# Spreading a vector over the partitions through DRAM instead of through TensorE, in a two-stage cross-attention kernel

## The chip, the cores and the metric

The kernel runs on one core of one Trainium2 chip. The metric is the device time of one execution in microseconds.

## What is computed

For 64 independent sequences: x is 256 x 512, the context c is 256 x 256, all in float32. Two cross-attention layers follow one another, the second one with its softmax over the query axis and a layer norm:

```
Q = x Wq0 + bq0; K = c Wk0 + bk0; V = c Wv0 + bv0
x1 = x + softmax(Q K^T / sqrt(512), axis = keys) V Wo0 + bo0
q = x1 Wq1 + bq1; k = c Wk1 + bk1; v = c Wv1 + bv1
w = softmax(q k^T / sqrt(512), axis = queries)
x2 = w v + x1
out = (x2 - mean) * rsqrt(var + eps) * gamma + beta
```

The kernel multiplies the weights together beforehand. The key bias bk1 then contributes a term x1 . g1 to the score of each query, with g1 = Wq1 bk1 / sqrt(512). It differs from query to query, so it does not drop out of a softmax over the queries, and it has to be added to each of the scores. The change is about this term.

## The kernel before

One round of the program works on several sequences at once, each in another stage. With r the round, TensorE (`body` in the PE block) issues u(r+3), Pc(r+2), g(r), S1(r), S0(r+3), pred(r-1), out(r+2), v(r+1), s(r), wc(r). The other engines have bodies of their own, written out by hand in program order: ScalarE (ACT) and GpSimd (POOL) split every operand of a matmul into a high and a low float32r part (`xT_h` and `xT_l`, and so on), VectorE (DVE) does the rest of the low parts, the maxima, the residual sums and the statistics. Rounds 4 to 55 are a loop of 13 trips of 4 bodies, the rest is unrolled. Engines wait for one another by semaphores only. Each engine's queue is strictly in order: a wait holds back all that stands behind it.

Two matrices are transposed by way of DRAM, through SyncE's (SP's) queue: `move_E0(n)` waits for E0_blk, writes it in four DMAs to E0_dram, waits for them and reads PT_raw back; `move_y(n)` does the same with y_blk, y_dram and yT_raw. PT_raw becomes PT_hi (ACT) and PT_lo (POOL), the moving operand of Pc; yT_raw becomes yT_hi and yT_lo, the moving operand of v. In round r SP does load_IN(r+5), load_x(r+2), store(r-2), move_E0(r+3), move_y(r+2). Before the rounds it runs move_E0(0), (1), (2) and move_y(0), (1).

The bias term: in round r DVE computes `dot(r+1)` (L729): for each half q of the queries, x1 times g1, summed along the row, into one column of gcol[n % 2] (128 x 2: one number per query). In the scores S1 the queries lie along the free axis and the keys on the partitions, so each of the 128 partitions needs all 256 numbers. PE's `g_` (L331) makes them: it transposes the column, broadcast to 128 x 128, against the identity `ident`, twice, into PSUM bank 0; ACT's `gT_` (L550) copies the 128 x 256 result to gT in SBUF; DVE's `max1` (L744) waits for gT and for S1, adds gT to both halves of S1 and takes the negative maxima.

```
last = nc.tensor.transpose(g_bank[:, q * P:(q + 1) * P],
                           gcol[n.k % 2][:, q:q + 1].to_broadcast([P, P]), ident[:, :])
...
copy(gT[:, 0, :], g_bank[:, 0:S]).then_inc(gT_set, 1)
```

In the profile's rows L268 is the helper `product`, from which nearly all matmuls come, L337 the transposes of `g_`, L475 ACT's copies, L735 the dots, L750 the addition of gT, L787 the sum x2, L908 POOL's low parts; SP's rows are L195 (R, that is load_x), L203 and L207 (move_E0), L214 and L218 (move_y), L224 (store).

Of the kernel before, what the change touches and what calls it, by code (L numbers as in the profile page):

```python
# [4 lines left out]
P = 128  # L5
NSEQ, S, D, L = 64, 256, 512, 256
# [42 lines left out]
def build(nc, x, packed, WqT0, bq0, WkT0, WvT0, bv0, Wo0, bo0, WqT1, WkT1, bk1, Wv1, bv1, gamma, beta, out):  # L49
# [6 lines left out]
    with ExitStack() as stack:  # L56
# [6 lines left out]
        def sem(name):  # L63
            return stack.enter_context(nc.semaphore(name))

        ident = sb("ident", [P, P])
        A0 = split("A0", [P, DT, L])
        Bv = split("Bv", [P, LT, D])
        A1 = split("A1", [P, DT, L])
# [37 lines left out]
        yT_raw = sb("yT_raw", [P, NB * ST, DT, 32])  # L107
        yT = split("yT", [P, NB * ST, DT, 32])
        gcol = [sb(f"gcol{n}", [P, ST]) for n in range(2)]
        gT = sb("gT", [P, 1, S])  # L110
        srow = sb("srow", [P, S], f32r)
        nmax0, Z0 = sb("nmax0", [P, ST]), sb("Z0", [P, ST])
        rz0 = [sb(f"rz0{n}", [P, ST]) for n in range(2)]
# [4 lines left out]

        E0_dram = nc.dram_tensor("E0_dram", (NB, 32, NB, ST * LT * 32), f32, kind="Internal").ap()
        y_dram = nc.dram_tensor("y_dram", (NB, 32, NB, ST * DT * 32), f32, kind="Internal").ap()  # L120

        bank = [stack.enter_context(nc.psum_tensor(f"bank{n}", [P, 512], f32)) for n in range(8)]
        g_bank = s_bank = bank[0]
        Pc_bank = v_bank = bank[1]
        u_bank = bank[2]
        g1_b = bank[3]
# [15 lines left out]
        PT_hi, PT_lo = sem("PT_hi"), sem("PT_lo")  # L142
        Pc_full, Pc_hi, Pc_lo = sem("Pc_full"), sem("Pc_hi"), sem("Pc_lo")
        out_full, x1_set = sem("out_full"), sem("x1_set")
        g_set, g_full, gT_set = sem("g_set"), sem("g_full"), sem("gT_set")
        y_blk_set, y_blk_out, yT_in = sem("y_blk_set"), sem("y_blk_out"), sem("yT_in")
        yT_hi, yT_lo = sem("yT_hi"), sem("yT_lo")
        v_full, v_hi, v_lo = sem("v_full"), sem("v_hi"), sem("v_lo")
# [29 lines left out]
        @block.sync  # L178
        def _(sp):
            def weights(dst, src, n):  # L180
                sp.dma_start(dst[:, :, :], src).then_inc(w_in[n], 16)

            def load_IN(n):
                if not n.there():
                    return
                first(sp, xT_lo, n.count(back=2))
                first(sp, cT_lo, n.count(back=2))
                first(sp, C_lo, n.count(back=2))
                sp.dma_start(IN[n.k % 2][:, :], packed[n.index()]).then_inc(in_in[n.k % 2], 16)

            def load_x(n):
                if not n.there():
                    return
                first(sp, Y_set, n.count(2, 1, back=4))
                sp.dma_start(flat(R[n.k % 4]), x_v[n.index()]).then_inc(x_in[n.k % 4], 16)  # L195

            def move_E0(n):
                if not n.there():
                    return  # L200
                sp.wait_ge(E0_blk_set, n.count())
                for i in range(NB):
                    sp.dma_start(E0_dram[:, :, i, :].rearrange("a m x -> m a x"),  # L203
                                 E0_blk[32 * i:32 * i + 32, :, :, :].rearrange("p a c t -> p a (c t)")
                                 ).then_inc(E0_out, 16)
                sp.wait_ge(E0_out, n.count(64, 63))
                sp.dma_start(flat4(PT_raw), E0_dram.rearrange("a m i x -> (a m) (i x)")).then_inc(PT_in, 16)  # L207

            def move_y(n):
                if not n.there():  # L210
                    return
                sp.wait_ge(y_blk_set, n.count())
                for i in range(NB):
                    sp.dma_start(y_dram[:, :, i, :].rearrange("a d x -> d a x"),  # L214
                                 y_blk[32 * i:32 * i + 32, :, :, :].rearrange("p a c t -> p a (c t)")
                                 ).then_inc(y_blk_out, 16)
                sp.wait_ge(y_blk_out, n.count(64, 63))
                sp.dma_start(flat4(yT_raw), y_dram.rearrange("a d i x -> (a d) (i x)")).then_inc(yT_in, 16)  # L218

            def store(n):  # L220
                if not n.there():
                    return
                sp.wait_ge(Y_done, n.count())
                sp.dma_start(o_v[n.index()], flat(Y[n.k % 2])).then_inc(y_out[n.k % 2], 16)  # L224

            weights(WqT0_s, WqT0, 0)
            weights(WkT0_s, WkT0, 1)
            load_IN(Seq(0))
            weights(WvT0_s, WvT0, 2)
            weights(Wo0_s, Wo0, 3)  # L230
            load_IN(Seq(1))
            weights(WqT1_s, WqT1, 4)
            weights(WkT1_s, WkT1, 5)
            load_x(Seq(0))
            weights(Wv1_s, Wv1, 6)
            load_x(Seq(1))
            load_IN(Seq(2))
            move_E0(Seq(0))
            load_IN(Seq(3))
            move_E0(Seq(1))  # L240
            load_IN(Seq(4))
            move_y(Seq(0))
            move_E0(Seq(2))
            move_y(Seq(1))

            def body(r):
                load_IN(r.plus(5))
                load_x(r.plus(2))
                store(r.plus(-2))
                move_E0(r.plus(3))  # L250
                move_y(r.plus(2))

            for r in range(0, LOOP_FROM):
                body(Seq(r))
            with sp.Fori(0, LOOP_TRIPS) as j:
                for k in range(4):
                    body(Seq(LOOP_FROM + k, j))
            for r in range(LOOP_FROM + 4 * LOOP_TRIPS, NSEQ + 2):
                body(Seq(r))
            sp.wait_ge(y_out[0], 16 * (NSEQ // 2))  # L260
            sp.wait_ge(y_out[1], 16 * (NSEQ // 2))

        @block.tensor
        def _(pe):
# [63 lines left out]
                                   lambda b, t: by_q(yT[b], t), DT)  # L328
                last.then_inc(v_full, 1)

            def g_(n):  # L331
                if not n.there():
                    return
                pe.wait_ge(g_set, n.count(2, 1))
                first(pe, s_lo, n.count(back=1))
                for q in range(ST):
                    last = nc.tensor.transpose(g_bank[:, q * P:(q + 1) * P],  # L337
                                               gcol[n.k % 2][:, q:q + 1].to_broadcast([P, P]), ident[:, :])
                last.then_inc(g_full, 1)

            def S1_(n):
                if not n.there():
                    return
# [7 lines left out]
            def s_(n):  # L351
                if not n.there():
                    return
                pe.wait_ge(w_lo, n.count())
                pe.wait_ge(gT_set, n.count())
                for t in range(ST):
                    for b in range(2):
                        last = nc.tensor.matmul(s_bank[:, 0:S], pick[:, :], w[b][:, t, :],  # L358
                                                start=(t == 0 and b == 0), stop=(t == ST - 1 and b == 1))
                last.then_inc(s_full, 1)  # L360
# [80 lines left out]
            u_(Seq(3))  # L441
            over_h(bank[5][:, :], wide(1), Wo0_s)
            v_(Seq(0))
            pe.wait_ge(const_set, 2)
            pe.wait_ge(pick_set, 2)
            pe.wait_ge(su_lo, 11)

            def body(r, u=True):
                if u:
                    u_(r.plus(3))  # L450
                Pc_(r.plus(2))
                g_(r)
                S1_(r)
                S0_(r.plus(3))
                pred_(r.plus(-1), 0)
# [17 lines left out]
        def _(act):  # L473
# [73 lines left out]
                first(act, S1_full, n.count(back=1))  # L547
                copy(flat(vT[0]), v_bank[:, :]).then_inc(v_hi, 1)

            def gT_(n):  # L550
                if not n.there():
                    return
                act.wait_ge(g_full, n.count())
                first(act, S1_sum, n.count(back=1))
                copy(gT[:, 0, :], g_bank[:, 0:S]).then_inc(gT_set, 1)

            def exps1(n):
                if not n.there():
                    return
# [86 lines left out]
            def body(r, prefix=True):  # L646
# [2 lines left out]
                    C_h(r.plus(3))  # L649
                    u_h(r.plus(3))  # L650
                Pc_h(r.plus(2))
                gT_(r)
                yT_h(r.plus(1))
                cT_h(r.plus(4))
                xT_h(r.plus(4))
# [18 lines left out]
        def _(dve):  # L674
# [54 lines left out]
            def dot(n, q):  # L729
# [1 line left out]
                    return  # L731
                dve.wait_ge(x1_set, n.count(2, 1))
                first(dve, g_set, n.count(2, q, back=1))
                first(dve, g_full, n.count(back=2))
                nc.vector.scalar_tensor_tensor(junk[q][:, :], R[n.k % 4][:, q, :], 1.0, g1_b[:, :], ALU.mult,  # L735
                                               ALU.mult, accum_out=gcol[n.k % 2][:, q:q + 1]).then_inc(g_set, 1)

# [6 lines left out]
            def max1(n):  # L744
                if not n.there():
                    return
                dve.wait_ge(gT_set, n.count())
                dve.wait_ge(S1_full, n.count())
                E1 = S1_bank[:, :].rearrange("p (a b) -> p a b", a=ST)
                nc.vector.tensor_tensor(E1, E1, gT[:, :, :].to_broadcast([P, ST, S]), ALU.add  # L750
                                        ).then_inc(S1_sum, 1)
                dve.wait_ge(S1_sum, n.count())
                nc.vector.tensor_reduce(nmax1[:, :], E1, AX.X, ALU.max, negate=True).then_inc(nmax1_set, 1)
# [109 lines left out]
            dve.wait_ge(b_in, 16 * 7)  # L863
            nc.vector.tensor_tensor(row[96:P, :], bank[5][96:P, :], row[96:P, :], ALU.add).then_inc(su_lo, 1)
            dve.wait_ge(su_hi, 8)
            dve.wait_ge(const_set, 5)
            nc.vector.scalar_tensor_tensor(bvK[:, :], fp(row_hi[:, :]), less[:, 0:1], row[:, :], ALU.mult, ALU.add
                                           ).then_inc(su_lo, 1)
            dot(Seq(0), 0)
# [36 lines left out]
        def _(pool):  # L906
# [43 lines left out]
            def finish(n):  # L950
# [6 lines left out]
                for q in range(ST):  # L957
# [1 line left out]
                    last = nc.gpsimd.tensor_tensor(y[:, q, :], y[:, q, :], beta_b[:, :], ALU.add)  # L959
                last.then_inc(Y_done, 1)  # L960

            nc.gpsimd.memset(ident[:, :], 0.0).then_inc(const_set, 1)
            pool.wait_ge(const_set, 1)
            nc.gpsimd.affine_select(out=ident[:, :], in_=ident[:, :], compare_op=ALU.not_equal, fill=1.0,
                                    base=0, pattern=[[-1, P]], channel_multiplier=1).then_inc(const_set, 1)
            nc.gpsimd.memset(less[:, :], 0.0).then_inc(const_set, 1)
            for n, p in enumerate((64, 97)):
                pool.wait_ge(const_set, 3 + n)
                nc.gpsimd.affine_select(out=less[:, :], in_=less[:, :], compare_op=ALU.not_equal, fill=-1.0,
                                        base=-p, pattern=[[0, 1]], channel_multiplier=1).then_inc(const_set, 1)  # L970
            xT_l(Seq(0))
# [76 lines left out]
```

## Time and profile before

| | us |
|---|---|
| median of 3 runs | 1254.4 |
| lowest and highest | 1252.03, 1256.06 |
| the profiled execution, its own time | 1254.56 |
| its span | 1252.8 |
| PE busy | 1212.8 |
| POOL busy | 927.1 |
| DVE busy | 892.0 |
| ACT busy | 700.2 |

The span is the time between the first and the last record of the profiled execution. The matmul times are modelled from a pipelined engine: one that is shown as 0.28 us long may start 0.12 us after its predecessor, so starts tell more than durations. The trace has no busy time for SP; its queue shows as DMA issues. "To landing" is the time from a DMA's issue to the semaphore that reports its data.

### The profile page before, as it was taken

Reading aid. Unit: us, or ns where it says so; the run is one execution under the profiler, and the core shown is the slowest. Engines: PE = TensorE matmul, PEld = TensorE weight load, DVE = VectorE, ACT = ScalarE, POOL = GpSimd, SP = SyncE. Lnnn points to the kernel's source line nnn. Section 1 sums busy time; section 2 is a strip of 40 time slices with the busy share of each in tenths; the row PEclk is TensorE's granted clock in tenths of the full one; section 3 lists DMA queues with packets and bytes.
Section 4 is the critical chain, followed back from the end, with each engine's and each line's share of the span. In section 5 each row is a group of like instructions: output and inputs, shape, how many; then the busy total and the mean of one; then the engine's idle time right before and its main releaser. Section 6 shows DMA issues by size and latency. Waiting matters only on the chain.

```text
span 1252.8 us, 25385 instructions
## 1 busy us (share of the span) xinstructions
PE 1212.8 (97%) x8304; PEld 1122.5 (90%) x8304; DVE 892.0 (71%) x1874; ACT 700.2 (56%) x1545; POOL 927.1 (74%) x713
## 2 busy tenths in 40 slices
PE   6989999999999999999999999999999999999984
PEld 5779999999999999999999999999999999999973
DVE  1457777777777777777777777777777777767763
ACT  2436565655656565565656566555656655565542
POOL 2436778778877877787787778778777877877664
PEclk8999999999999999999999999999999999999988
DMA  8346666656655665665666566556655655665431
GB/s 327 108 137 211 187 197 214 206 173 216 219 185 197 212 210 172 213 220 178 204 210 212 170 212 222 186 195 212 216 169 206 224 193 186 215 199 176 151 118 50
DMA packets 121727, 241.36 MB, mean 193 GB/s; under 512 B 13920, under 2 KB 79456, under 8 KB 113120
## 3 DMA queue, kind: packets, MB, share of 16 engines
q1 hardware_dynamic: 120816, 240.18, 57.6%
q10 hardware_dynamic: 880, 0.79, 0.2%
q8 instruction: 17, 0.28, 0.1%
q14 instruction: 14, 0.11, 0.0%
HBM read 157.03 MB, written 83.89 MB: 192 GB/s over the span
## 4 chain that ended last, share of the span: by engine, by line
PE 89%; DMA 3%; DVE 3%; POOL 2%; issue 2%; ACT 1%; SPq 1%; ACTq 0%; POOLq 0%; DVEq 0%
PE bank L268 82%; PE bank L385 2%; PE bank L358 2%; DMA beta_b<-in_beta 1%; PE bank L337 1%; DMA yT_raw<-y_dram 1%; DVE stats L795 1%; DMA y_dram<-y_blk 1%; SPq L214 1%; PE bank L395 1%; PE bank L401 1%; DVE R L787 0%; POOL Y L956 0%; POOL yT_lo L908 0%; DVE y_blk L725 0%
## 5 line engine op out<-in xcount | busy, mean ns | idle before, releaser
L908 POOL TENSOR_TENSOR PT_lo<-PT_raw,PT_hi 128x512 fp32r<-128x512 f32 x64 | 82.7, 1292 | 192.4 <-ACT PT_hi L475 192.4
L596 ACT ACTIVATE Y<-R,nmr,rstd 128x512 f32<-128x512 f32 x128 | 97.4, 809 | 184.1 <-POOL nmr L948 184.1
L908 POOL TENSOR_TENSOR xT_lo<-IN,xT_hi 128x1024 fp32r<-128x1024 f32 x64 | 154.2, 2409 | 24.3 <-ACT xT_hi L475 24.3
L908 POOL TENSOR_TENSOR yT_lo<-yT_raw,yT_hi 128x1024 fp32r<-128x1024 f32 x64 | 154.4, 2412 | 23.2 <-ACT yT_hi L475 23.2
L956 POOL TENSOR_TENSOR Y<-Y,gamma_b 128x512 f32<-128x512 f32 x128 | 162.4, 1289 | 3.7 <-ACT Y L596 3.7
L959 POOL TENSOR_TENSOR Y<-Y,beta_b 128x512 f32<-128x512 f32 x128 | 163.1, 1297 | 0.0
L268 PE MATMUL bank<-yT_hi,A_hi 128*128 128x256 f32 x512 | 146.6, 286 | 5.4 <-POOL yT_lo L908 5.4
L268 PE MATMUL bank<-yT_hi,A_lo 128*128 128x256 f32 x512 | 147.4, 288 | 0.0
L268 PE MATMUL bank<-yT_lo,A_hi 128*128 128x256 f32 x512 | 146.7, 286 | 0.0
L268 PE MATMUL bank<-xT_hi,A_hi 128*128 128x256 f32 x512 | 144.1, 281 | 0.0
L268 PE MATMUL bank<-xT_lo,A_hi 128*128 128x256 f32 x512 | 144.0, 281 | 0.0
L268 PE MATMUL bank<-xT_hi,A_lo 128*128 128x256 f32 x512 | 143.7, 281 | 0.0
L787 DVE TENSOR_TENSOR R<-bank,R 128x512 f32<-128x512 f32 x128 | 88.4, 690 | 76.6 <-PE bank L268 76.3
L510 ACT ACTIVATE uT_hi<-bank,c 128x256 fp32r<-128x256 f32 x128 | 53.7, 470 | 116.3 <-PE bank L268 116.3
L683 DVE SCALAR_TENSOR_TENSOR uT_lo<-bank,c,uT_hi 128x256 fp32r<-128x256 f32 x128 | 56.0, 480 | 75.2 <-ACT uT_hi L510 75.2
L268 PEld LDWEIGHTS bank<-yT_hi,A_hi 128*128 128x128 f32 x512 | 97.8, 191 | 9.6 <-POOL yT_lo L908 6.6
L268 PE MATMUL bank<-Bv_hi,PcT_hi 128*128 128x512 f32 x256 | 101.3, 396 | 1.2 <-DVE R L787 0.9
L268 PE MATMUL bank<-Bv_lo,PcT_hi 128*128 128x512 f32 x256 | 102.0, 399 | 0.0
L268 PE MATMUL bank<-V_lo,wcT_hi 128*128 128x512 f32 x256 | 101.5, 397 | 0.0
L268 PE MATMUL bank<-V_hi,wcT_lo 128*128 128x512 f32 x256 | 100.9, 394 | 0.0
L268 PE MATMUL bank<-V_hi,wcT_hi 128*128 128x512 f32 x256 | 100.6, 393 | 0.0
L268 PE MATMUL bank<-Bv_hi,PcT_lo 128*128 128x512 f32 x256 | 100.3, 392 | 0.0
(116 smaller groups left out, 4204.8 us busy)
## 6 DMA issues: line engine op xcount, KB each, us to landing
IN<-in_packed SPq DMA_DIRECT2D x64, 1024.0 KB, 5.7
R<-in_x SPq DMA_DIRECT2D x64, 512.0 KB, 6.3
y_dram<-y_blk SPq DMA_DIRECT2D x256, 128.0 KB, 2.4
yT_raw<-y_dram SPq DMA_DIRECT2D x64, 512.0 KB, 3.6
out<-Y SPq DMA_DIRECT2D x64, 512.0 KB, 3.4
E_dram<-E_blk SPq DMA_DIRECT2D x256, 64.0 KB, 1.8
PT_raw<-E_dram SPq DMA_DIRECT2D x64, 256.0 KB, 2.6
WqT_s<-in_WqT SPq DMA_DIRECT2D x2, 1024.0 KB, 11.3
```

What stands on the lines that cost most here:

```text
L214: sp.dma_start(y_dram[:, :, i, :].rearrange("a d x -> d a x"), y_blk[32 * i:32 * i + 32, :, :, :].rearrange("p a c t -> p a (c t)")).then_ ...
L268: last = nc.tensor.matmul(dst, stat(a, t), mov(b, t), start=(first and t == 0 and n == 0), stop=(t == k - 1 and n == 2))
L337: last = nc.tensor.transpose(g_bank[:, q * P:(q + 1) * P], gcol[n.k % 2][:, q:q + 1].to_broadcast([P, P]), ident[:, :])
L358: last = nc.tensor.matmul(s_bank[:, 0:S], pick[:, :], w[b][:, t, :], start=(t == 0 and b == 0), stop=(t == ST - 1 and b == 1))
L385: nc.tensor.matmul(dst, srow[:, q * P:(q + 1) * P], bvK[:, :], start=True, stop=False)
L510: nc.scalar.activation(uT[0][:, l, :], u_bank[:, l * S:(l + 1) * S], ACT.Identity, bias=c0[:, l:l + 1]).then_inc(u_hi, 1)
L596: nc.scalar.activation(Y[n.k % 2][:, q, :], R[n.k % 4][:, q, :], ACT.Identity, bias=nmr[:, q:q + 1], scale=rstd[:, q:q + 1]).then_inc(Y_se ...
L683: nc.vector.scalar_tensor_tensor(uT[1][:, l, :], u_bank[:, l * S:(l + 1) * S], c0[:, l:l + 1], fp(uT[0][:, l, :]), ALU.add, ALU.subtract). ...
L787: nc.vector.tensor_tensor(R[n.k % 4][:, q, :], pred_bank[q][:, :], R[n.k % 4][:, q, :], ALU.add).then_inc(x2_set, 1)
L908: return nc.gpsimd.tensor_tensor(dst, src, fp(hi), ALU.subtract)
L956: nc.gpsimd.tensor_tensor(y[:, q, :], y[:, q, :], gamma_b[:, :], ALU.mult).then_inc(Y_mul, 1)
L959: last = nc.gpsimd.tensor_tensor(y[:, q, :], y[:, q, :], beta_b[:, :], ALU.add)
```

## The change

The transposes on PE, ACT's copy and the identity are gone. SP writes gcol(n), 128 partitions x 2 numbers, to a 256-element tensor in DRAM, in the order of the queries, as 256 single elements (`write_g`), waits for it, and reads the 1 KB back to each of the 128 partitions (`spread_g`). gcol, g_dram, gT and their semaphores are doubled. The write stands between load_x and store in SP's round, one round ahead of its use, the read between store and move_E0.

```diff
-        gT = sb("gT", [P, 1, S])
+        gT = [sb(f"gT{n}", [P, 1, S]) for n in range(2)]
+        g_dram = [nc.dram_tensor(f"g_dram{n}", (ST, P), f32, kind="Internal").ap() for n in range(2)]
...
+            def write_g(n):
+                if not n.there():
+                    return
+                sp.wait_ge(g_set, n.count(2, 1))
+                sp.dma_start(g_dram[n.k % 2].rearrange("q p -> p q"), gcol[n.k % 2][:, :],
+                             allow_slow_non_contiguous=True).then_inc(g_out[n.k % 2], 16)
+
+            def spread_g(n):
+                if not n.there():
+                    return
+                sp.wait_ge(g_out[n.k % 2], n.landed(2))
+                sp.dma_start(gT[n.k % 2][:, 0, :], g_dram[n.k % 2].rearrange("(a q) p -> a (q p)", a=1)
+                             .to_broadcast([P, S])).then_inc(gT_in[n.k % 2], 16)
...
             move_E0(Seq(2))
+            write_g(Seq(0))
             move_y(Seq(1))
+            spread_g(Seq(0))
 
             def body(r):
                 load_IN(r.plus(5))
                 load_x(r.plus(2))
+                write_g(r.plus(1))
                 store(r.plus(-2))
+                spread_g(r.plus(1))
                 move_E0(r.plus(3))
                 move_y(r.plus(2))
...
-            def g_(n):
...
-                g_(r)
                 S1_(r)
...
             def s_(n):
                 if not n.there():
                     return
                 pe.wait_ge(w_lo, n.count())
-                pe.wait_ge(gT_set, n.count())
+                first(pe, s_lo, n.count(back=1))
...
-            def gT_(n):
...
-                gT_(r)
                 yT_h(r.plus(1))
...
             def dot(n, q):
...
-                first(dve, g_full, n.count(back=2))
+                first(dve, g_out[n.k % 2], n.landed(2, back=2))
...
             def max1(n):
...
-                dve.wait_ge(gT_set, n.count())
+                dve.wait_ge(gT_in[n.k % 2], n.landed(2))
```

How the instructions stand on SP, where the new steps lie. First SP's queue ahead of the rounds, before the change (rows that only name the buffers E0, y and their DRAM copies belong to move_E0 and move_y):

```order
L207 DMA PT_raw<-E0_dram 128x512 [waits E0_out]
L214 DMA y_dram<-y_blk 32x4x256 [waits y_blk_set]
L214 DMA y_dram<-y_blk 32x4x256 x3
L218 DMA yT_raw<-y_dram 128x1024 [waits y_blk_out]
L189 DMA IN1<-in_packed 128x2048 [waits C_lo,cT_lo,xT_lo]
```

And the same place now:

```order
L222 DMA PT_raw<-E0_dram 128x512 [waits E0_out]
L202 DMA g_dram0<-gcol0 128x2x1 [waits g_set]
L229 DMA y_dram<-y_blk 32x4x256 [waits y_blk_set]
L229 DMA y_dram<-y_blk 32x4x256 x3
L233 DMA yT_raw<-y_dram 128x1024 [waits y_blk_out]
L209 DMA gT0<-g_dram0 128x256 [waits g_out0]
L190 DMA IN1<-in_packed 128x2048 [waits C_lo,cT_lo,xT_lo]
```

The write of sequence 0, with its wait for the dots, now stands ahead of move_y(1), and the read behind it. Next the first of the loop's four bodies on SP, before the change (round 4; ISA and REGISTER_ALU rows count the semaphores' values):

```order
L195 DMA R2<-in_x 128x1024
L223 REGISTER_ALU
L224 ISA [waits Y_done]
L224 DMA out<-Y0 128x1024
L203 DMA E0_dram<-E0_blk 32x4x128 [waits E0_blk_set]
L203 DMA E0_dram<-E0_blk 32x4x128 x3
L206 ISA
L207 DMA PT_raw<-E0_dram 128x512 [waits E0_out]
```

And now:

```order
L196 DMA R2<-in_x 128x1024
L201 REGISTER_ALU
L202 DMA g_dram1<-gcol1 128x2x1 [waits g_set]
L238 REGISTER_ALU
L239 ISA [waits Y_done]
L239 DMA out<-Y0 128x1024
L208 ISA
L209 DMA gT1<-g_dram1 128x256 [waits g_out1]
L218 DMA E0_dram<-E0_blk 32x4x128 [waits E0_blk_set]
L218 DMA E0_dram<-E0_blk 32x4x128 x3
L221 ISA
L222 DMA PT_raw<-E0_dram 128x512 [waits E0_out]
```

The write stands between R and the store, the read between the store and E0_dram. Last PE's queue between Pc and S1 in round 0, before the change:

```order
L268 MATMUL bank1<-PT_hi,C2_lo 128x256
L337 MATMUL bank0<-ident,gcol0 128x128 [waits g_set]
L337 MATMUL bank0<-ident,gcol0 128x128
L268 MATMUL bank5<-vT_hi,cT0_hi 128x256 [waits v_lo]
L268 MATMUL bank5<-vT_lo,cT0_hi 128x256
```

Now the L337 rows are gone, and S1 follows Pc directly; nothing else has moved on PE.

## Rows read from the trace of the kernel before

**Rows 1.** The page: busy us of each engine; clock granted to TensorE, 40 slices.
```profile
PE 1212.8 (97%) x8304; PEld 1122.5 (90%) x8304; DVE 892.0 (71%) x1874; ACT 700.2 (56%) x1545; POOL 927.1 (74%) x713
...
PEclk8999999999999999999999999999999999999988
```

**Rows 2.** One round by windows: busy us per engine, PEclk, DMA share, GB/s.
```profile
600.44:618.68 18.24, 18.24 (x129) 17.07 (x129) 13.83 (x30) 10.80 (x25) 14.57 (x12) 1.00 0.62 206
```

**Rows 3.** The chain of waits, 600 to 640 us: start, length, what.
```profile
629.15 0.22 PE bank L337 x2
```

**Rows 4.** Timeline of PE at that place: start us, us, instruction.
```profile
628.87 0.28 PE L268 MATMUL bank<-PT_hi,C_lo 128*128 128x256 f32 x1
628.99 0.38 PE L337 MATMUL bank<-ident,gcol 128*128 128x128 f32 x2
629.13 0.36 PE L268 MATMUL bank<-vT_hi,cT_hi 128*128 128x256 f32 x1
629.33 0.28 PE L268 MATMUL bank<-vT_lo,cT_hi 128*128 128x256 f32 x1
```

**Rows 5.** Groups by line: ScalarE's copy of gT; busy us, mean ns, idle before.
```profile
L475 ACT ACTIVATE gT<-bank 128x256 f32<-128x256 f32 x64 | 24.2, 378 | 0.0
```

**Rows 6.** Timeline of SP in one round: start us, us, DMA issue.
```profile
628.26 0.34 SPq L195 DMA_DIRECT2D R<-in_x  x1
632.58 0.36 SPq L224 DMA_DIRECT2D out<-Y  x1
635.25 1.78 SPq L203 DMA_DIRECT2D E_dram<-E_blk  x4
638.37 0.34 SPq L207 DMA_DIRECT2D PT_raw<-E_dram  x1
641.66 1.75 SPq L214 DMA_DIRECT2D y_dram<-y_blk  x4
```

**Rows 7.** DMA issues over the span: count, KB each, median us to landing.
```profile
R<-in_x SPq DMA_DIRECT2D x64, 512.0 KB, 6.3
...
yT_raw<-y_dram SPq DMA_DIRECT2D x64, 512.0 KB, 3.6
...
E_dram<-E_blk SPq DMA_DIRECT2D x256, 64.0 KB, 1.8
...
PT_raw<-E_dram SPq DMA_DIRECT2D x64, 256.0 KB, 2.6
...
bcol<-in_bk ACTq DMA_DIRECT2D x1, 2.0 KB, 8.8
```

**Rows 8.** Timeline of ACT, POOL, PE and DVE around Pc and x2, same stretch.
```profile
623.91 0.63 ACT L475 ACTIVATE PT_hi<-PT_raw 128x512 fp32r<-128x512 f32 x1
...
624.62 1.29 POOL L908 TENSOR_TENSOR PT_lo<-PT_raw,PT_hi 128x512 fp32r<-128x512 f32 x1 [2.98 <-ACT PT_hi L475]
...
627.54 0.28 PE L268 MATMUL bank<-PT_hi,C_hi 128*128 128x256 f32 x1
...
635.54 0.69 DVE L787 TENSOR_TENSOR R<-bank,R 128x512 f32<-128x512 f32 x1 [0.27 <-PE bank L268]
```

**Rows 9.** Timeline of SP, DVE, ACT and PE where the rounds begin.
```profile
76.71 1.76 SPq L214 DMA_DIRECT2D y_dram<-y_blk  x4
...
80.44 0.34 SPq L218 DMA_DIRECT2D yT_raw<-y_dram  x1
...
80.87 0.08 DVE L735 DVE_READ_ACCUMULATOR junk<-R,bank 128x1 f32 x1
...
86.43 0.70 DVE L750 TENSOR_TENSOR bank<-bank,gT 128x512 f32<-128x512 f32 x1 [0.46 <-PE bank L268]
...
85.40 1.06 ACT L475 ACTIVATE yT_hi<-yT_raw 128x1024 fp32r<-128x1024 f32 x1
...
98.17 0.38 PE L268 MATMUL bank<-PT_hi,C_hi 128*128 128x256 f32 x1
```

**Rows 10.** The chain of waits, 1050 to 1160 us.
```profile
1102.99 3.68 DMA yT_raw<-y_dram
```

More of the change, by code:

```diff
@@ L64, in sem @@
             return stack.enter_context(nc.semaphore(name))
-        ident = sb("ident", [P, P])
         A0 = split("A0", [P, DT, L])
@@ L120, in build @@
         y_dram = nc.dram_tensor("y_dram", (NB, 32, NB, ST * DT * 32), f32, kind="Internal").ap()
+        g_dram = [nc.dram_tensor(f"g_dram{n}", (ST, P), f32, kind="Internal").ap() for n in range(2)]
         bank = [stack.enter_context(nc.psum_tensor(f"bank{n}", [P, 512], f32)) for n in range(8)]
-        g_bank = s_bank = bank[0]
+        s_bank = bank[0]
         Pc_bank = v_bank = bank[1]
@@ L144, in build @@
         out_full, x1_set = sem("out_full"), sem("x1_set")
-        g_set, g_full, gT_set = sem("g_set"), sem("g_full"), sem("gT_set")
+        g_set, g_out = sem("g_set"), [sem(f"g_out{n}") for n in range(2)]
+        gT_in = [sem(f"gT_in{n}") for n in range(2)]
         y_blk_set, y_blk_out, yT_in = sem("y_blk_set"), sem("y_blk_out"), sem("yT_in")
@@ L329, in v_ @@
                 last.then_inc(v_full, 1)
-            def g_(n):
[L332 to L339, printed above, removed]
             def S1_(n):
@@ L443, in _ @@
             v_(Seq(0))
-            pe.wait_ge(const_set, 2)
             pe.wait_ge(pick_set, 2)
@@ L548, in v_h @@
                 copy(flat(vT[0]), v_bank[:, :]).then_inc(v_hi, 1)
-            def gT_(n):
[L551 to L555, printed above, removed]
             def exps1(n):
@@ L746, in max1 @@
                     return
-                dve.wait_ge(gT_set, n.count())
+                dve.wait_ge(gT_in[n.k % 2], n.landed(2))
                 dve.wait_ge(S1_full, n.count())
                 E1 = S1_bank[:, :].rearrange("p (a b) -> p a b", a=ST)
-                nc.vector.tensor_tensor(E1, E1, gT[:, :, :].to_broadcast([P, ST, S]), ALU.add
+                nc.vector.tensor_tensor(E1, E1, gT[n.k % 2][:, :, :].to_broadcast([P, ST, S]), ALU.add
                                         ).then_inc(S1_sum, 1)
@@ L865, in _ @@
             dve.wait_ge(su_hi, 8)
-            dve.wait_ge(const_set, 5)
+            dve.wait_ge(const_set, 3)
             nc.vector.scalar_tensor_tensor(bvK[:, :], fp(row_hi[:, :]), less[:, 0:1], row[:, :], ALU.mult, ALU.add
@@ L960, in finish @@
                 last.then_inc(Y_done, 1)
[L962 to L965, printed above, removed]
             nc.gpsimd.memset(less[:, :], 0.0).then_inc(const_set, 1)
             for n, p in enumerate((64, 97)):
-                pool.wait_ge(const_set, 3 + n)
+                pool.wait_ge(const_set, 1 + n)
                 nc.gpsimd.affine_select(out=less[:, :], in_=less[:, :], compare_op=ALU.not_equal, fill=-1.0,
```

## The prediction, made before the changed kernel was run

 The windows by round say the same: a round lasts 18.24 us and PE is busy in all of it, POOL 14.57, DVE 13.83, ACT 10.80 [rows 2]. Then the chain of waits: from 160 to 1088 us it never leaves PE, and once a round it holds the piece that this change removes, two matmuls of L337, 0.22 us [rows 3]. So whatever leaves PE's stream there is worth its full time, until another chain becomes as long as 18.24 us. The question is what else comes near that.
>
> **Removed from PE.** Two transposes a round, 64 rounds. The timeline of PE shows the starts: 628.87 the last matmul of Pc, 628.99 and following the transposes, 629.13 the first of S1, 629.33 the second [rows 4]. Without the transposes the three steps from 628.87 to 629.33 (0.46 us) would be two of the usual 0.12, 0.24 us: 0.22 us a round, as the chain has it. The row of the pair shows 0.38 us of duration, but most of that overlaps its neighbours. I count the rounds in which the chain passes through L337: round 0 (0.27 us), rounds 1 to 55 (55 x 0.22 = 12.1), 59 to 61 (0.66) and 63 (0.40): 13.4 us. In rounds 56 to 58 the chain is not on PE: it runs through DVE, SP and the DMA of yT [rows 10], so nothing is gained there. A rule of the Trainium skill prices this otherwise: "TensorE: Matmul & The Clock Gate", section on PE-mode transpose, gives about 275 ns for a 128x128 transpose within a kernel; by it the pairs would be worth 128 x 0.275 = 35 us, and the sum would be 1222. The start-to-start times here speak for 0.22 us a pair; I take them.
>
> **Removed from ACT.** The copy of gT, 64 x 0.378 us = 24 us [rows 5]. ACT is busy 56%, and right after this copy it waits for yT_raw's DMA. Worth nothing.
>
> **Added on SP and the DMA engines, in each round.** Four steps: (1) after load_x the issue of write_g. Its semaphore is long set, the dots having run at the start of the same DVE round. An issue costs about 0.6 us of SP; until the store of Y at 632.58 SP had been waiting 4 us [rows 6], so this is free. (2) The write: 256 elements of 4 B. No row shows such a write. In the queue it stands behind R, issued at 628.26, which lands 6.3 us later, at 634.6 [rows 6, 7]. Lower end: it lands with R. Nearest row for a small write to DRAM: E_dram, 1.8 us from issue to landing with nothing ahead of it [rows 7], so 636.4 as a normal upper end. I take 635.4, about 6.5 us after its issue at 628.9. The far end is the only transfer with rows of 16 B, bcol, 8.8 us behind a full queue [rows 7]: 637.7. (3) SP waits for that landing, spread_g is issued (0.6 us), and only then move_E0, which waits behind it on SP: E_dram starts at 636.0 instead of 635.25, 0.75 us late (0 to 1.8 by the ends above). (4) The spread read, 128 KB in the same queue ahead of E_dram's packets: half of PT_raw's transfer, which takes 2.6 us in all, so 0.5 us at most beyond (3).
>
> What does the lateness of E_dram cost? PT_raw is issued 3.1 us after E_dram begins and lands 2.6 us after that: 641.0 [rows 6, 7]. ACT turns it into PT_hi at 623.91 in the previous round, so at 642.15 in this one: 1.2 us of slack. PT_lo ends at 625.91, PE starts Pc at 627.54: another 1.6 us [rows 8]. Together 2.8 us against 0.75, at most 2.3. Nor is y_dram reached: SP comes to it 2.9 us before y_blk is ready [rows 6]. **gT itself** lands some 3 us after the spread's issue, and max1 reads it a dozen us later. Cost in a round: nothing.
>
> **Added where the rounds begin.** Here the order matters: write_g(0) stands ahead of move_y(1) on SP and waits for dot(0), whose end is at 80.95; y_dram(1) was issued at 76.71 [rows 9]. Now it is issued at 81.4, 4.7 us late, and yT_raw(1) at 85.1 instead of 80.44; it lands (3.6 us) at 88.7 instead of 84.0. ACT took it at 85.40, so yT_hi(1) is 3.3 us late. spread_g(0) stands behind move_y(1), so gT(0) lands near 89.4 and DVE's add, at 86.43 before, is 3.0 us late. Both push the exponentials, E0_blk(3), PT_raw(3) and PT_lo(3), which PE needs for Pc(3) at 98.17 [rows 9], where PT_lo had ended 0.06 us earlier: no slack. I take +3.0 us once (0 if the waits swallow it, 4.7 if all comes through). From there on the schedule is the same, shifted.
>
> **At the end**: write_g(63) makes the store of Y(60) 0.6 us late, which nobody waits for; gT(63) is there 10 us before its use. Nothing. POOL's identity matrix goes from the setup: off the chain, nothing.
>
> **Sum**: 1254.6 (the profiled execution; the median of the runs is 0.2 lower) - 13.4 + 3.0 = 1244.2, against the median **1244.0 us**. With the start's ends 1241 to 1246.
>
> **Does PE stay the bound?** The next chain is yT_raw, ACT's three copies, exps0, E0_blk, x2, moments, w_l, x1, y_blk, y_dram, yT_raw. In each round it touches PE only where DVE waits for pred's second half, 0.27 us before x2 [rows 8], and at most as much again at E0_blk. So it could run about 0.3 to 0.6 us a round shorter; PE now gets 0.22 shorter. It fits, barely.
>
> **Rivals.**
> *A, the write lands late, slower.* It decides at 8.4 us after its issue (2.8 us of slack: E_dram at 638.0, spread at 637.4, and 628.9 from there). With bcol's 8.8 us the write lands at 637.7, E_dram begins at 638.3, 3.05 us late, and PE stands 0.24 us at each of 61 Pc: 15 us, and the time is 1254.6 - 13.4 + 3.0 + 15 = 1259. Each further us costs 61 more. For it: 256 packets of 4 B where each of E_dram's has 512 B, and a queue with 1.5 MB just ahead. Against it: E_dram's four issues are 512 packets and land in 1.8 us. The Trainium skill speaks for it: "DMA: Bandwidth & Descriptors" says in its rules for kernel authors that a strided last dimension becomes one descriptor per element, and in its specifications that under 512 B the engine reads, modifies and writes; no run here shows what that costs. Chance 0.16.
> *B, the yT chain becomes the bound, no change.* If it has no more than the 18.24 us it shows now, because another wait stands behind the 0.27 us, PE waits the 0.22 us that it saved; the start's 3.0 us remain: 1257.6 or, with part of the gain, 1251 to 1257. For it: in rounds 56 to 58 this chain already leads. Chance 0.11.
> *C, a pair of transposes costs its whole duration*, 0.38 us [rows 4]: 64 x 0.38 = 24.3, so 1254.6 - 24.3 + 3.0 = 1233. Against it: the starts. Chance 0.03.
>
> **How the numbers follow.** Forecast 0.70 (with 0.08 of it for a gain between 4 and 7 us). Faster by over 0.3% (3.8 us, about what a measurement of this kernel tells from no change): forecast and C, 0.73. Same: B, 0.11. Slower: A, 0.16. The range 1238 to 1262 leaves out C and the part of A beyond 9 us of landing, 0.11, together 0.14.
>
> **What would show it.** Right: the round in the windows goes from 18.24 to 18.02 us; S1's matmuls follow Pc's at 0.12 us; g_dram lands 6 to 7.5 us after issue; E_dram begins up to 2 us later against DVE's E0_blk, and PT_lo still ends before Pc; at the start yT_raw(1) is issued near 85 and Pc(3) near 101. Wrong: a wait of PE for PT_lo in every round (A), or for DVE's R with DVE's wait for pred gone (B), or a start that costs nothing.

## The result, and the profile after

The changed kernel takes 1661.7 us (median of 6 runs, 1656.2 to 1664.6) against 1254.1 us before: a ratio of 1.324 (95% interval 1.322 to 1.326), 32% slower. The prediction was 1244.0, range 1238 to 1262. The mechanism of rival A took place, with a far larger size, and on a closed ring of waits that rival A had not drawn.

The page of the changed kernel: busy times, TensorE's granted clock in 40 slices, and the shares of the chain of waits by line.

```profile
PE 1325.1 (80%) x8176; PEld 1223.8 (74%) x8176; DVE 889.2 (54%) x1874; ACT 683.7 (41%) x1481; POOL 920.1 (56%) x711
...
PEclk9979989899988998998998989988988988988997
...
DMA g_dram<-gcol 36%; PE bank L287 10%; DMA PT_raw<-E_dram 8%; DMA E_dram<-E_blk 8%; POOL PT_lo L907 4%; SPq L218 4%; POOL C_lo L907 3%; ACT PT_hi L482 2%; SPq L196 1%; SPq L190 1%; DVE stats L794 1%; SPq L209 1%; DMA beta_b<-in_beta 1%; DM
```

TensorE was 97% busy [rows 1]; now it is at 80%, and it holds 12% of the chain instead of 89%. The write of g alone holds 36%. The span grew by 405 us (1657.7 against 1252.8).
The windows, one round of the changed kernel (it answers to [rows 2]), and in PE's timeline the wait ahead of Pc:

```profile
826.84:851.57 24.73, 19.75 (x126) 18.37 (x126) 13.70 (x30) 10.58 (x24) 14.32 (x12) 0.93 0.63 154
```

```profile
826.82 0.39 PE L287 MATMUL bank<-PT_hi,C_hi 128*128 128x256 f32 x1 [4.10 <-POOL PT_lo L907]
```

A round lasts 24.73 us instead of 18.24, and in each one PE waits for PT_lo: 4.6 us in the median of the rounds between 300 and 1000 us (2.8 to 7.1). The chain of waits over this round (start, length, what), from one read of PT_raw to the end of the next E_dram:

```profile
821.90 2.87 DMA PT_raw<-E_dram
...
824.79 0.64 ACT PT_hi L482
...
825.49 1.00 POOL PT_lo L907
...
826.72 1.29 POOL C_lo L907
...
828.24 0.36 SPq L190
...
828.85 0.34 SPq L196
...
829.30 12.13 DMA g_dram<-gcol
841.44 0.32 SPq L209
...
841.81 0.42 SPq L218
...
843.25 3.38 DMA E_dram<-E_blk
```

This is a ring without TensorE. SP waits for g_dram's landing (12.1 us), issues the read and E_dram; E_dram lands, PT_raw is read, ACT and POOL make PT_hi and PT_lo; right behind PT_lo stands C_lo on POOL, and SP's load_IN of the next round waits for C_lo (L175); R and the next write of g follow. 7.40 us from PT_raw's issue to the write's, 12.14 for the write, 0.37 for the issue of the read, 4.82 for E_dram: 24.73 us. So the ring sets the period, and in this kernel whatever the write takes is paid in full.

The DMA issues of the changed kernel: count, KB each, median us to landing (answers to [rows 7]).

```profile
R<-in_x SPq DMA_DIRECT2D x64, 512.0 KB, 10.5
...
E_dram<-E_blk SPq DMA_DIRECT2D x256, 64.0 KB, 2.8
PT_raw<-E_dram SPq DMA_DIRECT2D x64, 256.0 KB, 2.9
gT<-g_dram SPq DMA_DIRECT2D x64, 128.0 KB, 3.7
```

R stands ahead of the write in the queue, and yet its landing grew from 6.3 to 10.5 us; E_dram, behind it, went from 1.8 to 2.8. Not all of R's growth is the write's doing; the kernel with eight rows, below, tells the parts.

### The profile page after: what moved, and what is told of

Its sections match the earlier page's. It is cut to its first block, busy times and chain, and to the rows that moved or that the text cites. A ratio compares the mean times of both kernels' runs of the same rounds, so it can differ in the third digit from the quotient of the medians.

```text
span 1657.7 us, 25127 instructions
## 1 busy us (share of the span) xinstructions
PE 1325.1 (80%) x8176; PEld 1223.8 (74%) x8176; DVE 889.2 (54%) x1874; ACT 683.7 (41%) x1481; POOL 920.1 (56%) x711
## 4 chain that ended last, share of the span: by engine, by line
DMA 54%; PE 12%; issue 12%; POOL 10%; SPq 8%; DVE 3%; ACT 2%; POOLq 0%; ACTq 0%; DVEq 0%
DMA g_dram<-gcol 36%; PE bank L287 10%; DMA PT_raw<-E_dram 8%; DMA E_dram<-E_blk 8%; POOL PT_lo L907 4%; SPq L218 4%; POOL C_lo L907 3%; ACT PT_hi L482 2%; SPq L196 1%; SPq L190 1%; DVE stats L794 1%; SPq L209 1%; DMA beta_b<-in_beta 1%; DMA y_dram<-y_blk 1%; POOL rstd L945 1%
## 5 line engine op out<-in xcount | busy, mean ns | idle before, releaser
L287 PE MATMUL bank<-PT_hi,C_hi 128*128 128x256 f32 x256 | 108.9, 425 | 289.0 <-POOL PT_lo L907 285.8
L287 PEld LDWEIGHTS bank<-PT_hi,C_hi 128*128 128x128 f32 x256 | 74.7, 292 | 302.7 <-POOL PT_lo L907 233.7
L675 DVE TENSOR_TENSOR wcT_lo<-bank,wcT_hi 128x512 fp32r<-128x512 f32 x64 | 44.3, 691 | 369.3 <-ACT wcT_hi L482 369.3
L482 ACT ACTIVATE PT_hi<-PT_raw 128x512 fp32r<-128x512 f32 x64 | 40.2, 629 | 378.9 <-DMA PT_raw<-E_dram 378.8
L716 DVE SCALAR_TENSOR_TENSOR R<-bank,rz,R 128x512 f32<-128x512 f32 x128 | 90.2, 746 | 39.7 <-DMA R<-in_x 37.1
L482 ACT ACTIVATE PcT_hi<-bank 128x512 fp32r<-128x512 f32 x64 | 38.2, 597 | 166.6 <-PE bank L287 166.6
L675 DVE TENSOR_TENSOR PcT_lo<-bank,PcT_hi 128x512 fp32r<-128x512 f32 x64 | 44.3, 691 | 108.3 <-ACT PcT_hi L482 108.3
## 6 DMA issues: line engine op xcount, KB each, us to landing
R<-in_x SPq DMA_DIRECT2D x64, 512.0 KB, 10.5
```

Of the source, the lines that this page charges most:

```text
L287: last = nc.tensor.matmul(dst, stat(a, t), mov(b, t), start=(first and t == 0 and n == 0), stop=(t == k - 1 and n == 2))
L482: return nc.scalar.activation(dst, src, ACT.Copy, **kw)
L675: return nc.vector.tensor_tensor(dst, src, fp(hi), ALU.subtract)
L716: nc.vector.scalar_tensor_tensor(R[n.k % 4][:, q, :], out_bank[q][:, :], rz0[n.k % 2][:, q:q + 1], R[n.k % 4][:, q, :], ALU.mult, ALU.add) ...
```

## The experiments

For each kernel with a write, L below is the time on SP's timeline from the issue of g's write to that of its read, which waits for the landing: the median of the rounds between 300 and 1000 us (28 of them in the changed kernel, up to 39 in faster ones). In the changed kernel L is 12.7 us (11.0 to 15.3).

**No DMA, no transposes.** What is the removal worth by itself?

```diff
-                write_g(r.plus(1))
...
-                spread_g(r.plus(1))
...
-                dve.wait_ge(gT_in[n.k % 2], n.landed(2))
...
+            nc.vector.memset(gT[0][:, 0, :], 0.0)
+            nc.vector.memset(gT[1][:, 0, :], 0.0)
```

> Leaves out the bias term: neither transposes nor the write and the read, gT is zeros set once, the rest is the changed kernel. It measures what the removal from PE is worth by itself. By my account of the removal (0.22 us a round on PE, 13.4 us over the chain): 1241 us, round 18.02 us. By rival B (the chain of yT takes over): 1248 to 1254. By the duration of a pair (0.38 us): 1230.

Measured: 1239.7 us (ratio 0.988, 0.987 to 0.990). Its windows:

```profile
600.44:618.46 18.02, 18.02 (x128) 16.84 (x128) 13.86 (x30) 10.53 (x23) 14.48 (x12) 1.00 0.62 204
```

The round is 18.02 us, to the digit what the start-to-start times of PE gave [rows 4], and PE is busy in all of it: the chain of yT does not take over. The total is 1.3 us better than my 1241. This kernel's chain stays on PE also in rounds 56 to 58, from which I had credited nothing. In the profiled execution its first round also begins 3.0 us earlier (PE's piece of the chain behind vT_lo starts at 78.74 instead of 81.71), but that is the setup's clock and not the change: the chain has 16 setup matmuls in 2.17 us instead of 3.57, with a granted clock of 0.79 instead of 0.50 between 20 and 22 us, and 60 later ones in 9.06 us instead of 10.23. The identity, which POOL no longer makes, is not on that chain. The removal was priced rightly; everything else is the cost of the two DMAs.

**Rows of 8 bytes.** 128 pieces instead of 256, in the same 1 KB; the order of the numbers in it is another, and the addition reads gT accordingly.

```diff
-            sp.dma_start(g_dram[n.k % 2].rearrange("q p -> p q"), gcol[n.k % 2][:, :],
-                         allow_slow_non_contiguous=True)
+            sp.dma_start(g_dram[n.k % 2], gcol[n.k % 2][:, :])...
...
```

> The two numbers of a partition are written as one row of 8 bytes, 128 rows instead of 256 elements; the sum over the addition reads gT in that order. If the write costs a turn for each row (in its DMA engine or at the DRAM), the landing falls from 12.5 us to 6 to 7 us after the issue, below the 8.4 us of slack, and the time falls to 1240 to 1260. If the 12.5 us are the queue ahead of it (1.5 MB) or a fixed cost of a write to DRAM, it stays at 12 us and 1640 to 1665.

Measured: 1441.4 us (1.151, 1.148 to 1.154), L = 9.4 us (8.4 to 10.1). One round on SP:

```profile
811.07 0.37 SPq L202 DMA_DIRECT2D g_dram<-gcol  x1
814.96 0.36 SPq L238 DMA_DIRECT2D out<-Y  x1
821.18 0.32 SPq L208 DMA_DIRECT2D gT<-g_dram  x1
```

Neither expectation is met: half as many pieces save 3.3 us, not 6. And at 9.4 us it should by rival A's formula (61 us for each us beyond 8.4) have cost 61 us beyond the gain, 1305; it cost 200 beyond the 1240 of the kernel without DMAs. The formula was wrong, too.

**Each element in a place of its own**, 512, 64 and 16 bytes apart, and a control.

```diff
-... g_dram{n}", (ST, P), f32 ...
+... g_dram{n}", (ST, P, P), f32 ...  # 512 bytes; (ST, P, 16): 64 bytes; (ST, P, 4): 16 bytes; (ST, P, 1): the control
...
-            sp.dma_start(g_dram[n.k % 2].rearrange("q p -> p q"), gcol ...
+            sp.dma_start(g_dram[n.k % 2][:, :, 0].rearrange("q p -> p q"), gcol ...
...
-            ... g_dram[n.k % 2].rearrange("(a q) p -> a (q p)", a=1) ...
+            ... gamma[0:S].rearrange("(a n) -> a n", a=1) ...
```

> Each of the 256 elements goes to a 512-byte row of its own in DRAM; the read takes 1 KB of gamma instead, so the addition gets other numbers, and its time is unchanged. If the 256 writes are slow because they meet in the same 1 KB of DRAM, the landing falls to 2 to 6 us behind its issue plus what is ahead, and the time to 1245 to 1300. If each element costs its engine a turn wherever it goes, landing 12 to 13 us, time 1640 to 1665.

> As the kernel with 512-byte rows, but each of the 256 elements goes to 64 bytes of its own: 16 KB of DRAM instead of 128 KB (or of 1 KB); the read again takes gamma, so other numbers are added. If what the compact write adds is that the DMA engines write into the same few bytes (16 elements to 64 bytes), 64 bytes apart is as good as 512: landing 7 to 8 us after the issue, time near 1320. If it is the size of the region, it stays between: 9 to 12 us, 1400 to 1600. If nothing in the place matters, 12.5 us and 1660.

> Each element goes to 16 bytes of its own, so four elements share 64 bytes, of four neighbouring partitions; the read takes gamma, so other numbers are added. With 64 and 512 bytes of pitch the read is issued 8.2 and 7.9 us after the write (median, 300 to 1000 us), with 4 bytes 12.6. If the extra time grows with the number of writes into the same 64 bytes: 9 to 10 us, time 1370 to 1450. If what hurts is only that different DMA engines write into the same 64 bytes, and neighbouring partitions go to one engine: 8 us, time 1320 to 1335.

> The control of the padded kernels: the write is the compact one of the changed kernel (4 bytes of pitch), the read takes gamma. If the reads of gamma made the padded kernels fast and not the pitch of the write, it is near 1325; if it is the pitch, landing 12 to 13 us and a time of 1640 to 1665.

| distance of the elements | L, us | time, us (one run each) |
|---|---|---|
| 512 bytes | 7.9 | 1322 |
| 64 bytes | 8.2 | 1333 |
| 16 bytes | 8.4 | 1345 |
| 4 bytes (control) | 12.2 | 1602 |

The landings of g_dram in the DMA issues of two of them, 64 bytes first:

```profile
g_dram<-gcol SPq DMA_DIRECT2D x64, 1.0 KB, 8.1
```

```profile
g_dram<-gcol SPq DMA_DIRECT2D x64, 1.0 KB, 12.2
```

The 512-byte kernel missed its upper expectation of 1300, the control its lower one of 1640; the other two are as one of their accounts had it, or close. So some 4 us of the 12.2 come from the elements' lying side by side, and nearly all of that is gone at 16 bytes already. The control is 60 us faster than the changed kernel (L 12.2 against 12.7 us, and 3.6 against 4.1 us from E_dram's first issue to PT_raw's), so the read of the just-written 1 KB has a share of its own, but the step from 1602 to 1345 is the pitch. That only writes of different DMA engines into the same bytes hurt would fit the 16-byte row better (1320 to 1335 expected, 1345 measured) than a cost for each neighbour in 64 bytes (1370 to 1450); it is not shown, since the trace doesn't say which DMA engine writes which element. Even far apart, the 256 elements leave the kernel at 1322; the eight rows, below, show that what is left there is no longer their number.

**The read behind move_E0.** Is it SP's wait?

```diff
                 store(r.plus(-2))
-                spread_g(r.plus(1))
                 move_E0(r.plus(3))
+                spread_g(r.plus(1))
```

> The read (with its wait for the write) stands behind move_E0 on SP instead of ahead of it. If only SP's wait is what costs, E_dram starts at its old time and the time is 1244 to 1255. If the write also holds the packets and the landings behind it in the same queue, E_dram lands with the write, 12.5 us after the write's issue and 4 us later than before, of which 2.8 are slack: 1.3 to 3 us a round, 1320 to 1430.

Measured: 1519.1 us (1.211, 1.207 to 1.216), beyond even the upper expectation. SP in one round (the read of g, behind PT_raw's, is left out):

```profile
805.08 0.38 SPq L202 DMA_DIRECT2D g_dram<-gcol  x1
...
811.46 1.80 SPq L218 DMA_DIRECT2D E_dram<-E_blk  x4
819.99 0.34 SPq L222 DMA_DIRECT2D PT_raw<-E_dram  x1
```

E_dram is now first issued 6.4 us after the write, with no wait for it, and still PT_raw can be read only 8.5 us after E_dram's first issue, against 3.1 before [rows 6]. The write holds up what stands behind it. With SP's wait about a third of the loss went (143 of the 422 us above the kernel without DMAs); the rest stays with the write. The chain of waits no longer names g_dram here: E_dram's landing holds 24% of it, PE's matmuls 23%, the two y transfers 5% each.

**Both DMAs on ScalarE's queue**, which held nothing else in these rounds.

```diff
+                    C_h(r.plus(3))
+                    spread_g(r)              # act.wait_ge, act.dma_start
                     u_h(r.plus(3))
                 Pc_h(r.plus(2))
+                write_g(r.plus(1))           # act.wait_ge, act.dma_start
```

> Both DMAs are issued by ScalarE on its own queue: the write right behind Pc's copy, the read (with its wait) a round later behind C's copy; SP's queue is that of the kernel before without its waits. The write is the same 256 elements. If the write's landing only holds back what stands in its own queue and SP's wait, E_dram lands at its old 1.8 to 2.6 us and the time is 1242 to 1256. If the write holds back what the same 16 DMA engines do for any queue, E_dram lands late as before, and the time is 1400 or more.

Measured: 1543.0 us (1.227, 1.224 to 1.230). SP's timeline, then R among the DMA issues:

```profile
804.57 2.19 SPq L203 DMA_DIRECT2D E_dram<-E_blk  x4
812.90 0.34 SPq L207 DMA_DIRECT2D PT_raw<-E_dram  x1
```

```profile
R<-in_x SPq DMA_DIRECT2D x64, 512.0 KB, 13.0
```

The lower bound of 1400 holds. SP's queue contains no DMA and no wait of g here, and E_dram takes 8.3 us until PT_raw all the same, R 13.0 to land. Up to 1500 us the chain has no g in it either: R's landing holds 17% of it, E_dram's 13%. A slow write in one queue delays the other queue. The Trainium skill says why it can ("DMA: Bandwidth & Descriptors", section on queues, rings and completion order): both queues run on the same 16 DMA engines, and a completion increment lands only after every earlier write from its engine, across its queues. By that rule the run agrees.

**The write ahead of load_IN**, with its 256 elements.

```diff
+                write_g(r.plus(1))
                 load_IN(r.plus(5))
                 load_x(r.plus(2))
-                write_g(r.plus(1))
```

> The changed kernel with its 256 elements, with one step moved: the write stands ahead of load_IN on SP, so that 1.5 MB less stand before it in the queue. If the 12 to 13 us of landing are the write's own, it lands 12 us after its issue again, but is issued 1.1 us earlier: 1590 to 1620. If about 6 us of it are the queue ahead, it lands 6 to 7 us after the issue: 1245 to 1300.

Measured: 1561.0 us (1.244, 1.242 to 1.247), L = 8.6 us (8.0 to 10.2). SP in one round, and R's landing:

```profile
809.70 0.38 SPq L202 DMA_DIRECT2D g_dram<-gcol  x1
...
818.10 0.33 SPq L209 DMA_DIRECT2D gT<-g_dram  x1
818.49 2.49 SPq L218 DMA_DIRECT2D E_dram<-E_blk  x4
826.57 0.34 SPq L222 DMA_DIRECT2D PT_raw<-E_dram  x1
```

```profile
R<-in_x SPq DMA_DIRECT2D x64, 512.0 KB, 13.3
```

Neither expectation is met. 4.1 of the 12.7 us go with the 1.5 MB ahead of the write; 8.6 stay with only yT_raw's 0.5 MB ahead. But what is gained on the write is lost behind it: R lands 13.3 us after its issue instead of 10.5, E_dram takes 8.1 us until PT_raw. That the write occupies the DMA engines for about the same stretch wherever it stands would explain this; it is not shown.

**Eight rows of 128 bytes.** The same numbers to the same 1 KB in the same place of the queue; DVE transposes them first.

```diff
+                    nc.vector.transpose(gblk[n.k % 2][:, :], gcol[:, :]).then_inc(g_blk_set, 1)
...
-            sp.dma_start(g_dram[n.k % 2].rearrange("q p -> p q"), gcol[n.k % 2][:, :], ...)
+            for q in range(ST):
+                sp.dma_start(g_dram[n.k % 2][q, :].rearrange("(i j) -> i j", j=32), gblk[n.k % 2][q:P:32, :])
```

> The dots go to two columns of a 128x32 tile; DVE transposes it in 32x32 blocks (some 0.15 us a round), and two DMAs write 8 rows of 128 bytes into the same 1 KB instead of 256 elements. The order on SP, the wait and the read are those of the changed kernel. If the cost goes by the number of pieces, the landing is that of R or of E_dram, 6 to 7 us after the issue, inside the 8.4 us of slack, and the time is 1240 to 1250. If any write under 512 bytes costs about 12 us, or the order on SP is what costs, it stays above 1400.

Measured: 1264.9 us (median of 6 runs, 1256.8 to 1275.9; ratio 1.006, 1.004 to 1.009), L = 6.0 us (5.7 to 7.9). Its windows, late and early in the span:

```profile
800.00:1000.00 200.00, 200.00 (x1402) 187.00 (x1401) 156.07 (x335) 116.23 (x254) 160.48 (x124) 1.00 0.64 209
```

```profile
200.00:300.00 100.00, 92.86 (x642) 85.64 (x641) 74.26 (x151) 53.70 (x118) 72.87 (x56) 1.00 0.61 198
```

This misses the expected 1240 to 1250, but 397 of the 407 us are gone, so the cost goes with how the write is cut into pieces, not with DRAM, the order on SP or the wait. By the Trainium skill ("DMA: Bandwidth & Descriptors", Specifications) an engine reads, modifies and writes where a transfer has under 512 bytes, so these 128-byte rows should be slow ones, too: no run shows a loss from them.

From 400 to 1000 us PE never waits. Earlier it does: between 200 and 300 us it is idle for 7 of 100. Two pieces of the chain of waits from that time:

```profile
186.12 8.29 DMA g_dram<-gblk
...
245.29 7.94 DMA g_dram<-gblk
```

The same eight rows have two landings. Between 120 and 310 us L is 8.0 us, R lands 8.4 us after its issue, and a round lasts 19.5 us: the ring sets the period. From 340 us on it is 6.0, 6.3 and 18.0 us. The write lands about when R does, both times. So the table above reads otherwise than it seems: the 256 elements with 16 to 512 bytes between them (L 7.9 to 8.4, with R at 8.2 to 8.4) are no slower than eight rows in such rounds. There the number of pieces shows no cost (it can hide behind R); 4-byte pieces side by side cost 4.2 to 4.7 us more, 8-byte ones 1.4. And of R's growth in the changed kernel, 6.3 to 10.5, half is there with eight rows, too. Why R lands at 8.4 while the ring sets the period is not shown.

**The start.** The same kernel, with the start put in order.

```diff
-            write_g(Seq(0))
             move_y(Seq(1))
+            write_g(Seq(0))
             spread_g(Seq(0))
```

> The kernel with transposed rows with one change: ahead of the rounds the write and the read of sequence 0 stand behind move_y(1), not around it. My account of the start (write_g(0) makes yT(1) late, 3 us, once): 1264.9 - 3 = 1262, or up to 5 us less. If the loss comes from the first twenty rounds alone, in which E_dram is late, no change: 1262 to 1268.

Measured: 1245.9 us (0.995, 0.993 to 0.997; the single runs spread from 1243.8 to 1256.1). The one line was worth 19 us, not 3 to 8. Its first stretch of SP:

```profile
80.71 0.34 SPq L240 DMA_DIRECT2D yT_raw<-y_dram  x1
81.53 1.16 SPq L209 DMA_DIRECT2D g_dram<-gblk  x2
```

yT_raw(1) is back at 80.7. In the kernel with the old order it came at 88.0. That made PT_raw(3) 4.8 us late (101.7 instead of 96.9), but it also put the rounds into the slower pattern, 19.5 us each instead of 18.0, and eleven rounds later PT_raw was 21.6 us late. So the lateness grew until about 320 us, and then stayed; what ended the pattern there is not shown. A late start that costs once in a kernel with slack can cost in every round in one whose ring is nearly as long as its period.

**Write early, read late.** Both ends of the wait loosened, start in order.

```diff
+                write_g(r.plus(1))
                 load_IN(r.plus(5))
                 load_x(r.plus(2))
-                write_g(r.plus(1))
                 store(r.plus(-2))
-                spread_g(r.plus(1))
                 move_E0(r.plus(3))
+                spread_g(r.plus(1))
```

> The kernel with transposed rows (8 rows of 128 bytes), and on SP the write stands ahead of load_IN, the read behind move_E0; ahead of the rounds both stand behind move_y(1). If what was left of the loss there (1264.9) was the write's wait behind 1.5 MB and its being ahead of move_E0 and move_y(1), the round is 18.02 us from the first to the last and the time is that without any DMA of the bias, 1240 to 1244. If small writes cost something wherever they stand, 1250 to 1265.

Measured: 1247.2 us (0.995, 0.994 to 0.997), the same as the run before and between the two expectations. It is 7.5 us above the kernel without DMAs; from 1115 us on its chain passes through the y and E transfers again, as before the change [rows 10]. What of those 7.5 us the small DMAs cause was not taken apart further. Either of these two is faster than the kernel before by 0.5%, and both still compute the whole.

**The ring, added up.** The other links of the ring are the time from PT_raw's issue to the write's, from the read of g to E_dram's first issue, and from there to PT_raw's next issue; all are medians from SP's timelines, 300 to 1000 us (the last row: 120 to 310 us).

| kernel | L | other links | sum | round measured | time, us |
|---|---|---|---|---|---|
| changed kernel | 12.7 | 11.9 | 24.6 | 24.7 | 1662 |
| control, 4 bytes | 12.2 | 11.3 | 23.5 | 23.7 | 1602 |
| rows of 8 bytes | 9.4 | 11.7 | 21.0 | 21.2 | 1441 |
| 16 bytes apart | 8.4 | 11.4 | 19.8 | 19.8 | 1345 |
| 64 bytes apart | 8.2 | 11.4 | 19.5 | 19.6 | 1333 |
| 512 bytes apart | 7.9 | 11.4 | 19.3 | 19.2 | 1322 |
| eight rows, early | 8.0 | 11.5 | 19.5 | 19.5 | |

The ring closes within 0.2 us in each of them. The time is then about 1240 + 61 x (round - 18.02): 1649, 1588, 1431, 1346, 1335 and 1310 us by the measured rounds, within 14 us of the times. In the changed kernel the other links have 0.5 us more, since E_dram is held up. With 11.4 us of other links the write may take 6.6 us, not 8.4.

## Why the prediction was wrong, point by point

- **Removed from PE**: 13.4 us expected, 14.7 measured in all. Right: the round went from 18.24 to 18.02 us, 0.22 us a pair. The 275 ns of the Trainium skill ("TensorE: Matmul & The Clock Gate", section on PE-mode transpose) agree with the duration of a transpose in this trace, 0.272 us, but not with what it costs in a stream of matmuls; by them it would have been 35 us. Rival C is refuted, and rival B, too: at 18.02 us PE is still busy all the time.
- **Step (2), the write's landing**: I took 6.5 us and 8.8 as the far end; it took 12.7. This is the step that failed. I took the nearest small write, E_dram, and bounded by bcol's rows of 16 bytes; but E_dram's pieces have 512 bytes, and bcol is a read of DRAM. No row showed small writes to DRAM, and then my upper end was no bound. In the case that I myself had marked as unknown, 0.16 was too little, and 1262 was no end that a row supported.
- **The threshold, 8.4 us** (8.5 by the prediction's own 637.4 - 628.9): 1.2 and 1.6 us of slack were read rightly on the way to Pc, but the way through PT_lo has a second exit. The rows of the kernel before show it (POOL's C_lo, then SP's next load_IN, which waits for it):

```profile
626.12 1.30 POOL L908 TENSOR_TENSOR C_lo<-IN,C_hi 128x512 fp32r<-128x512 f32 x1 [0.21 <-ACT C_hi L475]
```

```profile
627.66 0.36 SPq L189 DMA_DIRECT2D IN<-in_packed  x1
```

  PT_lo ends at 625.91 and C_lo starts 0.21 us later. C_lo ends at 627.42, and IN is issued 0.24 us after that, exactly as in the changed kernel, where SP does wait for C_lo (828.01, 828.24). So PT_lo had 0.2 us of slack there, not 1.6. Whoever is late there delays IN, R and with them the next write itself. I priced the lateness at 61 us for each us, which the ring confirms, but from the wrong point on: 6.6 us and not 8.4. Even my own 6.5 us of landing would have been inside by 0.1 us only.
- **"The write is waited for, and nothing else is touched"** was silent in my account: I counted the spread's packets ahead of E_dram, but not that a slow write holds up the landings around it in every queue. Without SP's wait ahead of E_dram the time is still 1519. The 0.5 us for the spread (hardly the half of 2.6 us that the prediction calls it) came out: in the padded kernels E_dram takes 3.6 us until PT_raw instead of 3.1.
- **The start**: the place was right, the size wrong. yT_raw(1) was to be issued at 85.1; it was at 91.87, since y_dram(1) had to land behind the slow write:

```profile
79.26 0.39 SPq L202 DMA_DIRECT2D g_dram<-gcol  x1
79.69 2.41 SPq L229 DMA_DIRECT2D y_dram<-y_blk  x4
91.87 0.34 SPq L233 DMA_DIRECT2D yT_raw<-y_dram  x1
92.25 0.43 SPq L209 DMA_DIRECT2D gT<-g_dram  x1
```

```profile
98.01 0.70 DVE L749 TENSOR_TENSOR bank<-bank,gT 128x512 f32<-128x512 f32 x1 [14.15 <-DMA gT<-g_dram]
```

  Here SP had issued nothing for 9 us ahead of the write (PT_raw at 69.37), and still y_dram's four DMAs behind it landed 10.9 us after their issue (median) instead of 2.4: the profile of the first write alone would have shown the slow step. DVE waited 14.15 us for gT(0). What this start adds to the 1661.7 is not measured by itself; with eight rows the old order cost 19 us.
- **Nothing at the end, nothing from ACT's copy**: nothing in the runs speaks against either, but no run tests them alone.

## What to carry to other kernels

Look at how a DMA's bytes are cut up, not only at how many there are: 1 KB as 256 pieces of 4 bytes side by side landed later than the 512 KB ahead of it, and a 32x32 transpose on DVE ahead of it, which made 8 rows of it, gave back 397 of 407 us. The same 256 pieces with 16 bytes or more between them gave back most of that, too. When an engine that issues DMAs is given a wait, follow everything behind it until the chain closes on the same engine; the slack that counts is the smallest on the ring, not that on the way to the busy engine. When two variants are compared, compare rounds of the same kind: one kernel had landings of 8 us in its first rounds and of 6 later. And where no row shows an operation, a bound from another kind of operation is no bound: give the mechanism that hangs on it the larger chance.

## What the runs showed of the hardware

- A write of 256 elements of 4 bytes side by side to one KB of DRAM is waited for 12.7 us behind 1.5 MB, and 8.6 us with 0.5 MB ahead. Eight rows of 128 bytes take 8.0 us behind the same 1.5 MB while the ring sets the period and 6.0 us otherwise, both times about as long as the 512 KB load just ahead of them.
- The elements' distance matters: 12.2 us at 4 bytes, 8.4 at 16, 8.2 at 64, 7.9 at 512 (one run each).
- While the write of 4-byte elements is under way, transfers ahead of it, behind it and in the other queue land late: R, the 512 KB load, 10.5 to 13.3 us after its issue, where it takes 8.4 with eight rows in a ring-bound round and 6.3 without any wait of the ring; E_dram until PT_raw 8.1 to 8.5 us instead of 3.1, where it is issued before the write has landed or right behind it.
- Two float32 transposes of 128 columns in a stream of matmuls take 0.22 us together, at the granted clock of 1.00.
